# A decoder layer with a delta-rule recurrence and a mixture of experts: MLP weights behind the experts' weights, GpSimd's store wait later, rows and gathers ahead, and constant matmuls on TensorE at the end

## The reference, cut to what matters

```python
xn = layernorm(x)
out = x + attn_layer(xn) + moe(xn)

def attn_layer(x):                      # 16 heads of 16 features
    a = layernorm(x) * g1 + b1_
    q, k, v, beta, g = ...              # projections of a; k is normalised
    for t in range(512):                # one state of 16 x 16 per sequence and head
        S = S * g_t
        S = S + beta_t * outer(k_t, v_t - k_t @ S)
        o_t = q_t @ S
    x = x + concat(o) @ Wo + bo
    h = layernorm(x) * g2 + b2_
    return x + gelu(h @ w1 + b1) @ w2 + b2

def moe(x):                             # 64 experts, the best 8 of each token, 128 places each
    y = silu(x_e @ w_gate[e]) * (x_e @ w_up[e]) @ w_down[e]
    return weighted_sum_of_experts(y) + shared_expert(x)
```

## Time and profile before

| | us |
|---|---|
| median of 3 runs | 1931.17 |
| lowest, highest | 1927.6, 1935.36 |
| the profiled execution, its own time | 1931.82 |
| its span in the trace | 1930.1 |
| outside the span | 1.7 |
| VectorE busy | 1742.8 |
| GpSimd busy | 1587.7 |
| TensorE (matmuls) busy | 1436.1 |
| ScalarE busy | 909.1 |

### The profile page before, as it was taken

The page is one execution under the profiler, slowest core; times in us unless marked ns, Lnnn a source line. Parts: engine busy times, 40 slices in busy tenths (PEclk is TensorE's granted clock), DMA queues, the critical chain, the costliest instruction groups (busy, mean ns, idle before and its releaser), DMA issues. The chain is left out here.

```text
span 1930.1 us, 31359 instructions
## 1 busy us (share of the span) xinstructions
PE 1436.1 (74%) x8802; PEld 1247.6 (65%) x8802; DVE 1742.8 (90%) x4967; ACT 909.1 (47%) x2609; POOL 1587.7 (82%) x1343
## 2 busy tenths in 40 slices
PE   6776777877854577667665668988898988789738
PEld 5665666766743566556554557877777877668637
DVE  3599999999999999999987988989999999988970
ACT  4545455556544644555542445555554454334303
POOL 5469999898998888788897788889898999897851
PEclk9878778878875788788776779999999999989868
DMA  8575345534456657855658322242223311111120
GB/s 174 149 178 116 69 97 125 133 75 96 95 124 150 155 132 164 217 132 130 165 132 222 74 61 64 84 118 69 57 60 102 87 54 49 57 50 49 40 53 13
DMA packets 337169, 201.24 MB, mean 104 GB/s; under 512 B 208227, under 2 KB 327717, under 8 KB 336997
## 3 DMA queue, kind: packets, MB, share of 16 engines
q1 hardware_dynamic: 318724, 168.43, 35.5%
q0 software_dynamic: 15616, 30.55, 7.2%
q10 hardware_dynamic: 2656, 0.26, 0.1%
HBM read 127.58 MB, written 71.60 MB: 103 GB/s over the span
## 5 line engine op out<-in xcount | busy, mean ns | idle before, releaser
L827 POOL TENSOR_TENSOR rp<-S,qs 128x2048 f32<-128x2048 f32 x113 | 519.8, 4600 | 89.3 <-DVE S L1138 63.7
L1123 DVE SCALAR_TENSOR_TENSOR vwin<-S,gwin,bank 128x256 f32<-128x256 f32 x1024 | 483.7, 472 | 0.3
L1138 DVE SCALAR_TENSOR_TENSOR S<-S,gwin,bank 128x256 f32<-128x256 f32 x1024 | 483.1, 472 | 0.3
L1128 DVE TENSOR_REDUCE nu<-vwin 128x16 f32<-128x272 f32 x1024 | 438.1, 428 | 0.3
L1132 DVE TENSOR_TENSOR bank<-nu,bank 128x256 f32<-128x256 f32 x1024 | 430.6, 421 | 0.6
L1773 PE MATMUL bank<-region 128*128 128x128 f32 x2048 | 288.2, 301 | 0.0
L1773 PEld LDWEIGHTS bank<-region 128*128 128x128 f32 x2048 | 273.1, 214 | 18.7 <-issue 18.0
L835 POOL TENSOR_TENSOR r<-rp 128x1024 f32<-128x1024 f32 x113 | 274.3, 2428 | 7.0
L1653 PE MATMUL bank<-xaT,wqkvg 128*128 128x128 f32 (+1 forms) x1792 | 242.1, 288 | 11.1 <-ACT xaT L1312 8.0
L1784 PE MATMUL bank<-region 128*128 128x256 f32 x1024 | 234.7, 383 | 0.0
L1653 PEld LDWEIGHTS bank<-xaT,wqkvg 128*128 128x128 f32 (+1 forms) x1792 | 216.2, 190 | 25.5 <-ACT xaT L1312 11.6
(11 more groups left out here) (158 smaller groups left out, 2329.6 us busy)
## 6 DMA issues: line engine op xcount, KB each, us to landing
qkv_d<-stg SPq DMA_DIRECT2D x192, 128.0 KB, 2.3
region<-in_L_ffn_w_gate SPq DMA_DIRECT2D x64, 192.0 KB
region<-in_L_ffn_w_up SPq DMA_DIRECT2D x64, 192.0 KB
region<-in_L_ffn_w_down SPq DMA_DIRECT2D x64, 192.0 KB
region<-in_L_attn_x SPq DMA_DIRECT2D x16, 512.0 KB, 7.6
region<-in_L_attn_x SPq DMA_DIRECT2D x32, 256.0 KB, 4.8
xw_d<-region SPq DMA_DIRECT2D x32, 256.0 KB, 3.5
acc_d<-region SPq DMA_DIRECT2D x32, 256.0 KB, 4.1
```

The source lines that it names most:

```text
L827: g.tensor_tensor(rp[:, :, :].rearrange("p (a v) d -> p a v d", v=DH), S[h][:, lo:lo + HS].rearrange("p t s (v d) -> p (t s) v d", v=DH), ...
L1123: m[G] = mark(v.scalar_tensor_tensor(products_of(I, s, G)[0], earlier(h, s, G).rearrange("p (v d) -> p v d", v=DH), gwin[:, I // NB2 & 1, ...
L1128: m[G] = mark(v.tensor_reduce(nu[:, G], products_of(I, s, G)[1], AX.X, ALU.add))
L1138: ins = v.scalar_tensor_tensor(S[h][:, s, G], earlier(h, s, G), gwin[:, I // NB2 & 1, G, 1, t:t + 1], outer[G], ALU.mult, ALU.subtract)
```

## The change

The table of sums: at I = 37 tiles 0 and 1 are added after steps 2 and 5; before it was after steps 0 and 4. In `first_rows` the rows of tiles 2 and 3 are issued right behind those of 0 and 1, once the gathers of xg[0] have landed; w2, the wait for the last scatter and the sums of tiles 0 and 1 come behind them. At I = 33 w1 is issued behind the 12 DMAs of the experts. GpSimd's wait for the store of oblk moves from ahead of the large product to ahead of the two last additions. At I = 23 and 31 (j = 7) the four gathers that stood at the start of the next iteration are issued in the middle of the second `reads`, behind a scatter. TensorE gets 22 matmuls of constants (the identity times a part of Wo) into a bank that nothing reads: 16 after the last step of the recurrence and ahead of the first `back_attn` of the last four tiles, 4 ahead of the first `back_T` and 2 behind it.

```diff
--- before.py
+++ after.py
@@ -109,6 +109,8 @@
 
 def sum_at(I, s):
     own, before = tiles_of(I), tiles_of(I - 1)
+    if I == FILL + 2:
+        return {2: 0, 5: 1}.get(s)
     at = {}
     if before and same_seg(before[-1], before[-1] - 1):
         at[1 if len(before) == 3 else 0] = before[-1] - 1
@@ -617,17 +619,16 @@
             def first_rows():
 
                 sp.wait_ge(y_done, UNITS_R + E)
-                for i in range(2):
+                for r in range(RT):
+                    sp.wait_ge(g_ld[0][r], 16 * (E // RT // 2))
+                for i in range(4):
                     back_rows(i)
                 sp.dma_start(w2_s, w2.rearrange("(c p) n -> p c n", p=P)).then_inc(mlp_ld, 16)
                 sp.wait_ge(sc_done, 16 * E)
-                for h in range(BUF):
-                    for r in range(RT):
-                        sp.wait_ge(g_ld[h][r], 16 * (E // RT // 2))
+                for r in range(RT):
+                    sp.wait_ge(g_ld[1][r], 16 * (E // RT // 2))
                 for i in range(2):
                     back_sums(i)
-                for i in range(2, 4):
-                    back_rows(i)
                 sp.sem_inc(rows_free, 1)
 
             for I in range(NI):
@@ -640,10 +641,10 @@
                     for i in range(BUF):
                         sp.wait_ge(r_stored[i], 64 * NB2)
                         sp.wait_ge(w_stored[i], 32 * NB2)
+                if X0 <= I < X1:
+                    experts(I - X0)
                 if I == ROUNDS_END + 1:
                     mlp_load()
-                if X0 <= I < X1:
-                    experts(I - X0)
                 if I == FILL:
                     first_rows()
                 if f is not None:
@@ -821,8 +822,6 @@
 
                 lo = half * HS
                 pool.wait_ge(rec_done, I * 2 + (3 + half))
-                if half == 0:
-                    pool.wait_ge(o_stored, min(I >> 3, NBLK - 1) * OST)
                 pool.wait_ge(act_staged, I + 1)
                 g.tensor_tensor(
                     rp[:, :, :].rearrange("p (a v) d -> p a v d", v=DH),
@@ -837,6 +836,8 @@
                 link(g.tensor_tensor(r1[:, :, 0:2], r1[:, :, 0:2], r1[:, :, 2:4], ALU.add))
                 a = r1[:, :, 0:2].rearrange("p (t s v) c -> p s v t c", t=HS, s=2)
                 o, t0 = read_cols(I)
+                if half == 0:
+                    pool.wait_ge(o_stored, min(I >> 3, NBLK - 1) * OST)
                 for s in range(2):
                     link(g.tensor_tensor(o[:, s, :, t0 + lo:t0 + lo + HS], a[:, s, :, :, 0], a[:, s, :, :, 1], ALU.add))
 
@@ -927,7 +928,7 @@
                     residual(i - 1)
                     route_lowered(i - 1)
                 back_roots(I, 0)
-                if X0 <= I and I + 1 < X1:
+                if X0 <= I and I + 1 < X1 and (j or I == X0):
                     gather(n + 1, (n + 1) % 2)
                 if X0 < I <= X1:
                     scatter(n * RT - 1, 3, 1 - h)
@@ -946,7 +947,11 @@
                         products(I, h)
                         scatter(n * RT + 2, 2, h)
                     else:
-                        reads(I, h, 1, j, lambda: scatter(n * RT + 2, 2, h))
+                        def rows_ahead():
+                            scatter(n * RT + 2, 2, h)
+                            if I + 2 < X1:
+                                gather(n + 2, n % 2)
+                        reads(I, h, 1, j, rows_ahead)
                 else:
                     reads(I, h, 0, j, lambda: back_roots(I, 2))
                     if 1 <= i <= NRT:
@@ -1916,9 +1921,19 @@
                     back_iteration(I, h, tiles_of(I), f)
                 if I == ROUNDS_END + 2:
                     mlp_bias_mm()
+            def keep_running(n):
+
+                for _ in range(n):
+                    mm(G0[:, 0:D], ident[:, :], wo_s[:, 0, :], start=True, stop=True)
+
+            pe.wait_ge(gelu_done, LAST * 2 + 1)
+            pe.wait_ge(rec_done, 2 * NT + 2)
+            keep_running(16)
             back_attn(LAST)
             back_attn(LAST + 1)
+            keep_running(4)
             back_T(LAST)
+            keep_running(2)
             for i in range(LAST, NT):
                 if i + 2 < NT:
                     back_attn(i + 2)
```

## The result

In nine pairs the changed kernel took 1916.32 us (median; 1910.99 to 1925.38) and the kernel before 1932.18 (1925.5 to 1936.92): a ratio of 0.992, interval [0.990, 0.994]. The interval of each later ratio is 2 to 4 us to either side, so a difference of under 3 us is not settled by the medians. About 15 us were gained where 26.9 were forecast. The profiled execution took 1918.32 us, its span is 1916.6.

A forecast was written before the change was run, and what follows sets the result against it. VectorE, which carries the recurrence, was taken to bound the kernel, with GpSimd also setting the pace from I = 24 to 37. Gains of 11.8 + 8.6 + 6.5 = 26.9 us from 1931.8 gave 1904.9 us, range 1893 to 1916.

The forecast's parts named there:

- part 2: Gathers issued earlier at I = 23 and 31: shorter scatter landing waits make GpSimd 6.9 us earlier, bounds 0 and 10.
- first stage: I = 24 to 38: the changes to w1, gathers, rows and sums together gain 11.8 us, bounds 0 and 28.4.
- part 4: Sums after steps 2 and 5 at I = 37: gains 3.15 us, less 0.9 at I = 38.
- Two engines set the pace: I = 24 to 37: VectorE and GpSimd both pace; what counts is how much earlier GpSimd gets.
- rival 1: GpSimd does not hold: all VectorE waits of I = 31 to 37 go, 42.6 us, giving 1889; chance 0.06.
- Part 1: w1 behind the experts' weights at I = 33: VectorE's 9.29 us wait for hidden values goes, at cost 0.
- rival 2: Landing waits stay, if loads and not gathers hold scatters up: the 6.9 us are 0, giving 1912; chance 0.17.
- Part 3: Rows of tiles 2 and 3 ahead at I = 35, 36: TensorE's DMA wait goes, GpSimd another 2.6 us earlier.
- Part 5: Store wait ahead of the last additions: gains 4.4 us at I = 41 and 4.16 at I = 57, sum 8.6.
- Part 6: 22 constant matmuls after the last step: TensorE's later work runs at 2.4 GHz, gaining 6.5 us, bounds -7.6 and 7.9.
- Rival 3: Repeats after the last step run at 1.2 GHz throughout: +7.6 in place of -6.5, giving 1919; chance 0.10.

The follow-up runs named there:

- w1_first: Changed kernel with w1 issued ahead of the weights of the last four experts again: 0.9919 of the kernel before.
- less_gpsimd: Changed kernel without the largest of GpSimd's three additions in the first half of iterations 26 to 30, some outputs not computed: 1907.9 us.
- small_loads: Changed kernel with the weight loads of experts 16 to 63 cut to a small part: 1893.23 us.
- rows_back: Changed kernel with the rows of tiles 2 and 3 issued last again at I = 35: 0.9928 of the kernel before.
- sums_back: Changed kernel with the sums of tiles 0 and 1 after steps 0 and 4 again: 0.9951 of the kernel before.
- controls: Changed kernel run again unchanged beside other runs: 0.9932 and 0.9923 of the kernel before.
- short_windows: Changed kernel with the loads of the gates of block 6 cut to 2 of 128 partitions: 1910.96 us.
- best_2: Changed kernel with the scatter ahead of the store at I = 24 and 32, 20 repeats, second sums of I = 43 and 45 after step 5: 0.9892, 1908.91 us.

## Why the prediction was wrong

The direction was right; 1916.3 us lies just outside the range of 1893 to 1916. The step that failed most is part 2: the scatters' landing waits were put down to the gathers in front of them and forecast to go, 6.9 us, and they stayed. Two terms were mis-sized besides: 4.4 us at I = 41, which came back as waits from I = 43 on, and the repeats, 6.5 for a measured 1.6 to 3.8.

Undone one at a time, the parts are worth, against the changed kernel and with 2 to 4 us to either side: w1 last -1.2 us, gathers 1.2, rows 0.6, sums 5.0, the store wait 11.8 (of which some 7 only because the gathers were moved), repeats 2.5. So of the first stage's gain nearly all is part 4. Step by step:

- **Two engines set the pace (right).** A wait of VectorE was not counted at its length in I = 31 to 37, and rival 1 was kept small. w1_first and less_gpsimd show it. Missed was the tighter link: VectorE adds up rx of iteration I in iteration I+1, so the 9.29 us turned into 8.08 us in the same iteration. Part 1 alone is worth nothing (0.9919 without it).
- **Part 2, "I take both down to about 0.2" and "I take 2.0 off" (the step that failed most).** 6.9 us were forecast; the first 1/std came 0.9 us earlier against the start of I = 24 (1116.05 - 757.9 = 358.2, before 1114.86 - 755.8 = 359.1), and 1.7 and 2.4 us later in the two other traces of the changed kernel. At I = 24 and 32 the store took the gathers' place in front of the scatter, and with the store behind it 4.2 us were gained; elsewhere the loads on the other queue hold the landing up. The wait at I = 33 did fall, by 4.0 us, but those at I = 32 and 34 grew by 2.2 and 1.3, and the 64 scatters wait as long in sum as before. The prediction had named under 3 us as the mark of **rival 2**, and it is rival 2 that happened: of its two candidates, gathers or loads, small_loads picked the loads. The Trainium skill ("DMA: Bandwidth & Descriptors", section "Queues, rings and completion order") says that a completion lands only after all earlier writes of that DMA engine, whatever the queue. The runs agree with it: 2.0 us of wait on average with the loads, 0.2 without them, on a queue that carries none of them. They would also agree with transfers that merely share the engines. The prediction gave this rival 0.17.
- **Part 3 (mechanism right).** The DMA wait went and a wait for GpSimd's 1/std stayed; from the first 1/std to that of tile 2 it is 19.3 us, before 21.5, a gain of 2.2 where 2.6 were forecast. But by the medians of rows_back the whole part is worth 0.6 us, give or take 3.
- **Part 4 (undersized).** 3.15 - 0.9 were forecast; sums_back gives 5.0, as the sum of tile 0 had become late too.
- **Part 5, the 4.4 us of I = 41 (wrong) and the 4.2 of I = 57 (right).** The wait of I = 41 went, and I = 38 to 46 still takes the same time, with a wait of 2.29 to 4.82 us at I = 43 in its place and 3.37 to 4.18 at I = 45 (3.41 before). "0.6 of VectorE's wait stays" was measured at 0.37, and the three additions, estimated at 4.0, took 4.2 (2.36, 1.27 and 0.61), but the step stopped there and did not ask what was late two iterations on. What caps that stage, SyncE's queue or something else, stays open: short_windows could not tell, and best_2 lost half of its gain there as well. Unseen was that the part also protects part 2, worth about 7 us.
- **Part 6 (right in kind, mis-sized).** 6.5 were forecast for the tail; the traces show 3.8 and the medians 1.6 to 2.5. The step "eight at 1.04 and eight at 0.52: 12.5 us, to 1879.6" failed: the level rose 2.9 us into the repeats (5.0 and 5.2 in the controls), they took 8.6 to 9.7 us in place of 12.5 and ended 2.0 to 3.1 us before the rows, and the level fell again. Rival 3 did not occur.
- **The marks of the prediction.** As named: no hidden-values wait in I = 33, no wait over 1 us in I = 41 and 57, no idle product at block ends, 46.3 us from the first product of the last tiles to the end (45 forecast). Against: gates' wait 5.98, scatter waits 3.08 and 4.00.

In sum the terms 11.8 + 8.6 + 6.5 became about 4.2 + 4.2 + 3.8, and 2.3 us lie in stages without a changed line, no more than traces of one program differ there.

## What to carry to other kernels

When two engines run an iteration apart, list every semaphore by which the faster waits for the slower, with its iteration offset, before crediting it with a wait removed; then follow the gain through the next few iterations. A move in a queue swaps what stands in front, so ask what takes the place, and what the moved work used to cover where it was. A landing wait needs all transfers under way on the same DMA engines in the sum, not only those of its own queue.

## What the hardware showed

- A scatter's landing on q0 depends on q1. With the expert loads, the first scatters of I = 25 to 29 waited 0.4 to 3.0 us, 2.0 on average over three traces, behind a product of 4.5 us; without them 0.17.
- Two scatters, of which the second waits for the landing of the first, were never less than 4.5 us apart in the twenty traces, of which the issue is 1.6; in the run without the loads the least is 4.6 (1081.6 to 1086.2 us).
- The clock of TensorE can rise and fall within one short wait. In all traces the level rose 2.9 to 5.8 us into the repeats. In ten traces 16 repeats were followed by 1.9 to 3.1 us of idle time, and the level fell to 0.50 at 12.0 to 13.6 us after the last step; the tail was 58.1 to 59.9 us. In five traces with 1.67 to 1.80 us of idle time, and in three with 20 repeats, it stayed at 1.00, and the tail was 55.8 to 56.4. The fifteen traces of the first two groups are of kernels with the same program on TensorE from the last step on, so what such repeats bring can differ by 2 to 4 us without an edit to them. That the idle time decides it fits all these traces; it was varied only by the 20 repeats.
